# A graph layer with kernel attention: queries, keys and values taken after the first two row tiles, h kept in the place of x

## The chip, the cores and the metric

The kernel runs on one core of a Trainium2 chip. The metric is the device time of one execution in microseconds (us). Engines are named as the profile names them: PE is TensorE, DVE is VectorE, ACT is ScalarE, POOL is GpSimd, SP is SyncE, which here only issues DMAs. Each engine works through its own instructions in the order in which the program was written, and waits on semaphores.

## The reference

All of it is float32. `x` has 1250 rows (nodes) of 512 features, and there are 20000 edges, sorted by destination.

```python
h = relu(layernorm(x))                       # by row
xn = batchnorm1(h)                           # over the nodes
agg = segment_sum(xn[src], dst) / max(deg, 1)
conv = relu(agg @ W_conv + b_conv)
q, k, v = h[:256] @ Wq, h[:256] @ Wk, h[:256] @ Wv      # 8 heads of 64; only 256 positions exist
qf = exp(u(q) - diag(q) - rowmax) / 16 + 1e-6           # u = head @ proj.T, 256 features; diag = |q|^2 / 2
kf = exp(u(k) - diag(k) - max over positions and features) / 16 + 1e-6
attn = (qf @ (kf.T @ v)) / (qf @ sum(kf) + 1e-6)
h_attn = (attn @ Wo)[pos]                    # rows past 255 take row 255
out = x + batchnorm2(conv + h_attn + h)
```

Queries, keys and values need the first 256 rows of `h` alone, which are the first two tiles of 128 rows.

## The kernel before

The rows of `x` lie in ten tiles of 128 (the last has 98 rows). Loops over `i` run over these tiles, loops over `f` over four blocks of 128 features. Everything is written out by hand: the order of each engine's program is the order of its calls in the source.

**The layer norm.** DVE takes mean and variance of each tile (`ln_stats`, L832 to L837) in three groups (tiles 0 and 1; 2 to 5; 6 to 9), ACT takes the root (`ln_std_of`, L402), DVE makes scale and bias from it (`ln_scale`, L802 to L806 and L843). ACT writes h = relu(scale * x + bias) in float32 (`ln_tile`, L384) into `hring`, a ring of two tiles. From there ACT makes `h1`, the float16 of 2048 h (L389), DVE makes `h2`, the float16 rest (`split`, L848), and PE transposes the tile into a PSUM bank (`transpose_h`, L514), which ACT stores to `hT` (`store_hT`, L367). `hring` has two places, so that tile i waits until tile i-2 is split and transposed.

**Queries, keys, values.** PE multiplies columns 0 to 255 of `hT` with `wq` and `wk` (`qk`, L522, two calls each) and with `wvo` (L620). ACT stores q and k and squares them (L394, L397), from which PE takes the diagonals (`diagonal`, L550).

**The edges.** DVE counts for each window of ten destinations how many sampled edges lie below it (L821, L823, L824), PE adds this up (L506, bank "first"), DVE turns it into row numbers (L876, L879), and four indirect DMAs of POOL gather the edges (L355). DVE decodes them (L891 to L904), PE transposes the result (L570, bank "cols"; L574, bank "out"), and DVE copies that to `bcol` and `vcol` (L912, L913). Then, for each of 25 groups of windows, DVE makes two blocks of one-hot rows (`one_hots`, L870, two instructions), PE multiplies them (`count`, L537, ten matmuls) into bank 0 or 1, and ACT stores the counts (`store`, L376) to the adjacency `A16`. Aggregation is then a dense product of h1 and h2 with `A16` (`aggregate`, L611), in three chunks of 500, 500 and 250 destinations.

**The features and the attention.** PE makes u for keys (eight calls of `features` with `kT`, L629), ACT copies each (L445), DVE takes its maximum (L958), and the maxima of all keys go through PE ("kmaxT", L653; "kmax", L657). For the queries DVE takes the row maxima from the bank (`q_bias`, L992, L993), ACT takes the exponentials (L467, L468 for queries, L460 for keys), PE transposes them (`transpose_qf`, L639) into bank 7 for even heads and bank 2 for odd ones, and DVE (L1000, even) or ACT (L455, odd) stores them. A loop over pairs of heads `hp` = 0 to 3 holds this part on PE and DVE. After it PE runs `aggregate(0, FT)`, which sums the in-degrees and waits until ten groups are stored, then `aggregate(0, 0)`, then the attention (L681, L695, L709, L722) between further aggregations, and at last the convolution (L772), its batch norm and the transposes back (L787). `finish` adds x and SP writes the output.

**The first batch norm.** Its sums come from `hT` (`bn_piece`, L855, twelve instructions, and L938 to L941). Its scale and shift are made of them with a root from ACT (L437) and eight short instructions on DVE (L802 to L806, L949 to L951). `mean` (L984, L987) uses them.

**PSUM.** A list `order` gives each result its bank. `pe_open` waits until the last reader of that bank is done.

```python
            def ln_tile(i):
                if i >= 2:
                    act.wait_ge(h_split, i - 1)
                    act.wait_ge(full(("hT", i - 2)), uses[("hT", i - 2)][1])
```

## Time and profile before

| what | value |
|---|---|
| time, median of 3 runs | 210.41 us (209.47 to 214.38) |
| the profiled execution | 210.1 us |
| its span, first to last instruction | 208.3 us |
| mean granted clock of TensorE | 0.959 of full |
| PE busy | 174.3 us (84%) |
| DVE busy | 151.1 us (73%) |
| ACT busy | 73.9 us (35%) |

Busy is the time in which an engine has an instruction under way; matmuls overlap, so that a busy PE is not one at its peak. All times in the rows are counted from the span's start. 1.8 us of the profiled execution lie outside of the span.

### The profile page before, as it was taken

To read this page: it belongs to the slowest core of one execution; us is meant where nothing else is said; L and a number is where in the kernel's file an instruction comes from. 1 tells how busy PE (TensorE), PEld (TensorE's weight loads), DVE (VectorE), ACT (ScalarE), POOL (GpSimd) and SP (SyncE) were. 2 spreads that over 40 slices of the span, in tenths; PEclk is the share of its full clock that TensorE was granted. 3 is DMA by queue.
4 is the path that set the end of the run, shared out by engine and by line. 5 is a ranking of instruction groups with operands and counts; after the bars stand their busy time and mean duration, and the time that the engine had idled before them with its cause. 6 is when DMAs were issued, how large, how long until landed. Compare 5 with 4: busy or idle time off the path is not lost.

```text
span 208.3 us, 2829 instructions
## 1 busy us (share of the span) xinstructions
PE 174.3 (84%) x1072; PEld 122.8 (59%) x1072; DVE 151.1 (73%) x316; ACT 73.9 (35%) x139; POOL 6.8 (3%) x21
## 2 busy tenths in 40 slices
PE   0149989999939758999999999999986999998191
PEld 0127879756827544599956875555873444466190
DVE  5799989596989695077699989997760435265794
ACT  2074695953739893022112112111000212223560
POOL 5250000000000000000000000000000000000000
PEclk9999999999995996999999999999999999999769
DMA  5999500002300000000000000000000000000058
GB/s 187 337 322 354 192 0 3 0 0 74 148 0 0 0 5 0 0 3 0 3 0 0 0 3 0 0 3 0 0 3 5 0 0 0 3 0 0 2 203 289
DMA packets 6507, 11.13 MB, mean 53 GB/s; under 512 B 1050, under 2 KB 1376, under 8 KB 6492
## 3 DMA queue, kind: packets, MB, share of 16 engines
q1 hardware_dynamic: 6300, 10.67, 15.0%
q0 software_dynamic: 192, 0.26, 0.4%
q8 instruction: 10, 0.16, 0.4%
q14 instruction: 5, 0.04, 0.1%
HBM read 8.36 MB, written 2.56 MB: 52 GB/s over the span
## 4 chain that ended last, share of the span: by engine, by line
PE 73%; DVE 16%; ACT 6%; issue 3%; POOL 1%; DVEq 0%; ACTq 0%; POOLq 0%
PE bank L611 22%; PE bank L772 16%; PE bank L522 6%; PE bank L537 4%; PE bank L695 4%; PE bank L620 3%; PE bank L681 3%; PE bank L722 3%; DVE mxk L958 2%; PE bank L629 2%; DVE mxq L992 2%; PE bank L787 2%; DVE xs L1192 2%; PE bank L639 2%; PE bank L550 2%
## 5 line engine op out<-in xcount | busy, mean ns | idle before, releaser
L611 PE MATMUL bank<-r,h 128*128 128x500 f16 (+1 forms) x240 | 43.7, 339 | 0.0
L772 PE MATMUL bank<-r,wc 128*128 128x500 f32 (+1 forms) x96 | 33.8, 513 | 2.5 <-issue 2.5
L376 ACT ACTIVATE r<-bank 128x500 f16<-128x500 f32 x25 | 14.8, 591 | 54.1 <-PE bank L537 54.0
L611 PEld LDWEIGHTS bank<-r,h 128*128 128x128 f16 x240 | 23.0, 97 | 17.6
L772 PEld LDWEIGHTS bank<-r,wc 128*128 128x128 f32 x96 | 18.0, 189 | 18.1 <-issue 17.4
L487 ACT ACTIVATE r<-bank,vec 128x500 f32<-128x500 f32 (+1 forms) x12 | 7.3, 608 | 41.7 <-PE bank L772 41.7
L870 DVE TENSOR_TENSOR ohb<-iota,bcol 128x1280 f16<-128x1280 f16 x25 | 20.5, 819 | 2.0 <-PE bank L537 1.8
L522 PE MATMUL bank<-hT,r 128*128 128x256 f32 x64 | 16.9, 424 | 0.7 <-issue 0.7
L870 DVE TENSOR_TENSOR ohv<-iota,vcol 128x1000 f16<-128x1000 f16 x25 | 16.8, 671 | 0.0
L537 PEld LDWEIGHTS bank<-ohv,ohb 128*128 128x128 f16 x250 | 13.9, 101 | 3.6 <-issue 1.3
L537 PE MATMUL bank<-ohv,ohb 128*128 128x100 f16 x250 | 15.8, 210 | 0.0
L522 PEld LDWEIGHTS bank<-hT,r 128*128 128x128 f32 x64 | 13.5, 216 | 3.3 <-issue 1.1
L1159 DVE SCALAR_TENSOR_TENSOR r<-hT,haT,r 128x244 f32<-128x244 f32 (+2 forms) x12 | 6.7, 562 | 9.8 <-ACT r L487 9.8
L787 PE MATMUL bank<-ident,r 128*128 128x128 f32 (+1 forms) x40 | 6.9, 353 | 5.2 <-DVE r L1186 5.2
L984 DVE SCALAR_TENSOR_TENSOR r<-bank,s,r 128x500 f32<-128x500 f32 (+1 forms) x12 | 7.8, 648 | 3.9 <-PE bank L611 3.8
L514 PE MATMUL bank<-ident,hring 128*128 128x128 f32 x40 | 6.5, 307 | 4.8 <-ACT hring L384 4.8
L639 PE MATMUL bank<-ident,qe 128*128 128x128 f32 x32 | 6.2, 337 | 4.5 <-ACT r L455 4.4
L787 PEld LDWEIGHTS bank<-ident,r 128*128 128x128 f32 (+1 forms) x40 | 6.6, 188 | 5.6 <-DVE r L1186 5.6
L1158 DVE TENSOR_TENSOR r<-r,hT 128x256 f32<-128x256 f32 x4 | 1.7, 426 | 11.2 <-ACT r L487 11.2
L848 DVE SCALAR_TENSOR_TENSOR h<-hring,h 128x512 f16<-128x512 f32 x10 | 6.7, 683 | 3.2 <-ACT h L389 3.2
L384 ACT ACTIVATE hring<-xs,lnw 128x512 f32<-128x512 f32 x10 | 8.0, 803 | 2.5 <-DVE lnw L843 2.5
L1033 DVE COPY kv<-bank 128x260 f32<-128x260 f32 x4 | 1.7, 428 | 9.4 <-PE bank L681 9.4
(158 smaller groups left out, 260.6 us busy)
## 6 DMA issues: line engine op xcount, KB each, us to landing
xs<-in_x SPq DMA_DIRECT2D x9, 256.0 KB, 3.6
out<-xs SPq DMA_DIRECT2D x9, 256.0 KB
r<-in_L_gnn_Wq SPq DMA_DIRECT2D x1, 1024.0 KB, 7.0
r<-in_L_gnn_Wk SPq DMA_DIRECT2D x1, 1024.0 KB, 9.3
wvo<-in_L_gnn_Wv SPq DMA_DIRECT2D x1, 1024.0 KB, 11.5
wc<-in_L_gnn_W_conv SPq DMA_DIRECT2D x1, 1024.0 KB, 14.5
wvo<-in_L_gnn_Wo SPq DMA_DIRECT2D x1, 1024.0 KB, 5.3
xs<-in_x SPq DMA_DIRECT2D x1, 196.0 KB
```

What stands on the lines that cost most here:

```text
L376: act.activation(A16[:, :, p * GW * W:(p + 1) * GW * W].rearrange("p a (q d) -> p q a d", q=GW), bank[p % 2][:, 0:GW * NT * W].rearrange(" ...
L384: act.activation(hring[:, i % 2, :], xs[:, i, :], ACT.Relu, bias=lnw[:, 3, i:i + 1], scale=lnw[:, 2, i:i + 1]).then_inc(h_ready, 1)
L487: act.activation(yT[:, f, c0:c0 + cn], acc[:, 0:cn], ACT.Relu, bias=vec[:, 4 * V_BC + f:4 * V_BC + f + 1]).then_inc(read(("conv", c, f)), 1)
L522: last = nc.tensor.matmul(acc[:, t * NA:(t + 1) * NA], w[:, f, c:c + P], hT[:, f, 0:NA], start=(f == 0), stop=(f == FT - 1))
L537: last = nc.tensor.matmul(bank[p % 2][:, q * NT * W:(q + 1) * NT * W], ohb[:, s, :], ohv[:, s, :], start=(k == 0), stop=(k == K - 1))
L611: last = nc.tensor.matmul(acc[:, 0:cn], lhs, A16[:, s, c0:c0 + cn], start=(s == 0 and hh is not h2), stop=(s == NT - 1 and hh is not h1))
L639: last = nc.tensor.transpose(acc[:, o:o + P], qe[:, h % 4, t, m * P:(m + 1) * P], ident[:, :])
L695: last = nc.tensor.matmul(acc[:, j * (DH + 1):(j + 1) * (DH + 1)], qfT[:, m, h, t * P:(t + 1) * P], kv[:, m, h, :], start=(m == 0), stop=( ...
L772: last = nc.tensor.matmul(acc[:, 0:cn], wc[:, f, o * P:(o + 1) * P], aggT[:, f, c0:c0 + cn], start=(f == 0), stop=(f == FT - 1))
L787: last = nc.tensor.transpose(acc[0:n, f * P:(f + 1) * P], yT[:, f, i * P:i * P + n], ident[:, :])
L870: last = V.tensor_tensor(oh[:, s0:s0 + n, :].rearrange("p s (m t) -> p s m t", t=2), iota16[:, 0:size].rearrange("p (m t) -> p m t", t=2). ...
L984: V.scalar_tensor_tensor(out=aggT[:, f, c0:c0 + cn], in0=acc[:, 0:cn], scalar=s1[:, f:f + 1], in1=rdeg[:, c0:c0 + cn], op0=ALU.mult, op1=A ...
```

## The change

`hring` goes. `ln_tile` writes h over the tile of `xs` that held x. PE transposes and DVE splits from there, no tile waits for an earlier one, and the making of `h1` is a function of its own (`high_part`), called later. SP loads x once more once all tiles are transposed, halved and split, and `finish` waits for that. `asum`, which lay over `hring`, gets its own place.

On PE both calls of `qk` for the queries follow the first two transposes, then come the other tiles by pairs with one product between two pairs: the keys' two, then the first half of the values. "first" stands behind the first two transposes, "cols" and "out" behind those of tiles 6 and 7. SP loads Wq after two tiles of x and Wk after six. Of the first four calls of `count` one stays before the features of the keys, three go between them.

On DVE the layer norm of tiles 0 and 1 comes ahead of L823 and L824, all layer norms come ahead of the decoding of the edges, the splits of tiles 6 to 9 move into the loop over `hp`, the sums of the first batch norm move behind that loop, and its scale and shift stand behind the attention's last result.

The diff, without the bank list, the helpers that only change a name, and lines that repeat (the `...` lines mark what is left out):

```diff
@@ SP
+            def load_x(i):
                 n = P if i < NT - 1 else LAST
+                sp.dma_start(xs[0:n, i, :], x[i * P:i * P + n, :]).then_inc(x_in[i], 16)
+            load_x(0)
+            load_x(1)
+            sp.dma_start(wq, w_q.rearrange("(t p) n -> p t n", p=P)).then_inc(wq_in, 16)
+            for i in range(2, 6):
+                load_x(i)
+            sp.dma_start(wk, w_k.rearrange("(t p) n -> p t n", p=P)).then_inc(wk_in, 16)
...
+            landed(sp, ("hT", NT - 1))
+            sp.wait_ge(h1_ready, NT)
+            sp.wait_ge(h_split, NT)
+            for i in range(NT):
+                load_x(i)
@@ ACT
             def ln_tile(i):
-                if i >= 2:
-                    act.wait_ge(h_split, i - 1)
-                    act.wait_ge(full(("hT", i - 2)), uses[("hT", i - 2)][1])
-                act.activation(hring[:, i % 2, :], xs[:, i, :], ACT.Relu,
+                act.activation(xs[:, i, :], xs[:, i, :], ACT.Relu,
                                bias=lnw[:, 3, i:i + 1], scale=lnw[:, 2, i:i + 1]).then_inc(h_ready, 1)
-                if i not in (0, 2):
-                    store_hT(i - 1)
+            def high_part(i):
                 act.wait_ge(h_ready, i + 1)
...
             ln_tile(2)
             ln_tile(3)
-            ln_std_of(2)
             qk(0, 0)
+            qk(0, 1)
+            store_hT(2)
+            store_hT(3)
             ln_tile(4)
             ln_tile(5)
-            qk(0, 1)
+            ln_std_of(2)
...
-                if h == 2:
+                if h in (1, 3, 5):
                     store()
...
+            store()
+            act.wait_ge(bn_var, 1)
+            act.activation(bw[:, 1, :], bw[:, 0, :], ACT.Sqrt).then_inc(bn_std, 1)
             while stores[0] < NGRP:
                 store()
@@ PE
             qk("q", wq, 0)
+            qk("q", wq, 1)
             transpose_h(2)
             transpose_h(3)
-            qk("q", wq, 1)
+            pe.wait_ge(wk_in, 16)
+            qk("k", wk, 0)
+            transpose_h(4)
+            transpose_h(5)
...
+            qk("k", wk, 1)
+            transpose_h(6)
+            transpose_h(7)
...
                 last.then_inc(full(("v", t)), 1)
+                diagonal(0, t)
                 diagonal(1, t)
-                count()
+                if t == 0:
+                    transpose_h(8)
+                    transpose_h(9)
+                    count()
...
                 features("uk", kT, i)
-                if i == 1:
+                if i in (1, 3, 5):
                     count()
             features("uq", qT, 0)
             features("uq", qT, 1)
-            count()
...
-                if hp < 3:
+                count()
+                if hp == 1:
                     count()
             aggregate(0, FT)
@@ DVE, the loop over hp and behind it
-                if hp < 3:
+                one_hots()
+                if hp == 1:
                     one_hots()
+                if hp == 0:
+                    split(6)
+                    split(7)
+                if hp == 1:
+                    split(8)
+                    split(9)
+            bn1_sums()
...
                 if i % 2:
                     one_hots()
+            bn1_scale()
             in_degrees(0)
             mean(0, 0)
...
             def finish(i):
                 n = P if i < NT - 1 else LAST
                 acc = landed(dve, ("zT", i))
+                dve.wait_ge(x_in[i], 32)
```

What the lists of instructions show at three places follows. First DVE at the start, from the comparison of the sampled edges (L821 before, L840 changed) on. `r<-r` is the work on the edges, `st<-xs`, `mv<-st` and `lnw` are the layer norm. Before:

```order
L821 TENSOR_TENSOR r<-r,thr 125x1250
L823 TENSOR_REDUCE r<-r 125x125
L824 COPY r<-r 125x250
L876 TENSOR_SCALAR first<-bank 126x2
L879 TENSOR_SCALAR rows<-first,rowc 126x2
L832 BN_STATS st<-xs 128x6 x2
L835 BN_AGGR mv<-st 128x2 x2
```

Changed:

```order
L840 TENSOR_TENSOR r<-r,thr 125x1250
L849 BN_STATS st<-xs 128x6 x2
L852 BN_AGGR mv<-st 128x2 x2
...
L860 SCALAR_TENSOR_TENSOR lnw<-mv,lnw 128x2
L894 TENSOR_REDUCE r<-r 125x125
L895 COPY r<-r 125x250
L849 BN_STATS st<-xs 128x6 x4
L852 BN_AGGR mv<-st 128x2 x4
L854 TENSOR_SCALAR lnw<-mv 128x4
L898 TENSOR_SCALAR first<-bank 126x2
L901 TENSOR_SCALAR rows<-first,rowc 126x2
```

The first layer norm has moved ahead of the edges' four instructions, and the row numbers behind the second group's statistics.

Second, PE from the last product of the keys to the features of the keys (`bank<-pT,r`); `bank<-half,r` are the diagonals, `bank<-ohv,ohb` one `count`. Before:

```order
L522 MATMUL bank<-hT,r 128x256 x8
L550 MATMUL bank<-half,r 128x2 x4
L537 MATMUL bank<-ohv,ohb 128x100 x10
L514 MATMUL bank<-ident,hring 128x128 x8
L620 MATMUL bank<-wvo,hT 128x512 x4
L550 MATMUL bank<-half,r 128x2 x4
L537 MATMUL bank<-ohv,ohb 128x100 x10
L620 MATMUL bank<-wvo,hT 128x512 x4
L550 MATMUL bank<-half,r 128x2 x4
L537 MATMUL bank<-ohv,ohb 128x100 x10
L629 MATMUL bank<-pT,r 128x256 x4
```

Changed:

```order
L527 MATMUL bank<-ident,xs 128x128 x8
L605 MATMUL bank<-ident,r 128x124
...
L635 MATMUL bank<-wvo,hT 128x512 x4
L563 MATMUL bank<-half,r 128x2 x8
L527 MATMUL bank<-ident,xs 128x128 x8
L550 MATMUL bank<-ohv,ohb 128x100 x10
L635 MATMUL bank<-wvo,hT 128x512 x4
L563 MATMUL bank<-half,r 128x2 x8
L648 MATMUL bank<-pT,r 128x256 x4
L550 MATMUL bank<-ohv,ohb 128x100 x10
L648 MATMUL bank<-pT,r 128x256 x4
```

"cols" (L605) now stands directly ahead of the values, and one `count` is left ahead of the features.

Third, DVE in the loop over `hp`, from the maxima of heads 6 and 7 (`mxq<-bank`) to the store of the transposed features of head 4 (`r<-bank 128x2x256`). Before:

```order
L992 TENSOR_REDUCE mxq<-bank 128x2
L993 SCALAR_TENSOR_TENSOR qb<-mxq,diag 128x2
L870 TENSOR_TENSOR ohb<-iota,bcol 128x1280
L870 TENSOR_TENSOR ohv<-iota,vcol 128x1000
L1000 TENSOR_SCALAR r<-bank 128x2x256
```

Changed, beginning with the splits of tiles 6 and 7 (`h<-xs,h`):

```order
L865 SCALAR_TENSOR_TENSOR h<-xs,h 128x512 x2
L1013 TENSOR_SCALAR r<-bank 128x2x256
...
L1005 TENSOR_REDUCE mxq<-bank 128x2
L1006 SCALAR_TENSOR_TENSOR qb<-mxq,diag 128x2
L887 TENSOR_TENSOR ohb<-iota,bcol 128x1280
L887 TENSOR_TENSOR ohv<-iota,vcol 128x1000
L887 TENSOR_TENSOR ohb<-iota,bcol 128x1280
L887 TENSOR_TENSOR ohv<-iota,vcol 128x1000
L865 SCALAR_TENSOR_TENSOR h<-xs,h 128x512 x2
L1013 TENSOR_SCALAR r<-bank 128x2x256
```

Four splits and one more pair of one-hot rows stand ahead of the store of head 4, which frees bank 7 for the transposes of head 6.

## Rows read from the trace of the kernel before

**Rows 1.** The page, the chain that ended last: shares of the span by engine.

```profile
PE 73%; DVE 16%; ACT 6%; issue 3%; POOL 1%; DVEq 0%; ACTq 0%; POOLq 0%
```

**Rows 2.** Timeline of DVE: start, duration, line, operation; in brackets idle time and releaser.

```profile
5.17 1.46 DVE L823 TENSOR_REDUCE r<-r 125x125 f32<-125x1250 f32 x1
...
8.57 1.28 DVE L832 BATCH_NORM_STATS2 st<-xs 128x6 f32<-128x512 f32 x2
```

**Rows 3.** Timeline of ACT, tiles 0 and 1.

```profile
12.68 0.63 ACT L389 ACTIVATE h<-hring 128x512 f16<-128x512 f32 x1
13.22 0.80 ACT L384 ACTIVATE hring<-xs,lnw 128x512 f32<-128x512 f32 x1
```

**Rows 4.** Issue of Wq by SP, and its size and time to landing.

```profile
3.02 0.43 SPq L312 DMA_DIRECT2D r<-in_L_gnn_Wq  x1
...
r<-in_L_gnn_Wq SPq DMA_DIRECT2D x1, 1024.0 KB, 7.0
```

**Rows 5.** Timeline of PE, 15.9 to 60 us.

```profile
15.92 6.07 PE L522 MATMUL bank<-hT,r 128*128 128x256 f32 x16 [0.73 <-issue]
...
22.70 3.62 PE L522 MATMUL bank<-hT,r 128*128 128x256 f32 x16
...
28.56 0.21 PE L581 MATMUL bank<-ident,vrow 20*128 20x20 f32 x1 [0.62 <-DVE vcol L913]
...
45.03 0.61 PE L537 MATMUL bank<-ohv,ohb 128*128 128x100 f16 x10
45.48 3.66 PE L620 MATMUL bank<-wvo,hT 128*128 128x512 f32 x8
...
50.33 1.14 PE L629 MATMUL bank<-pT,r 64*128 64x256 f32 x8
```

**Rows 6.** Timeline of DVE, 50 to 60 us.

```profile
51.77 0.17 DVE L802 RECIPROCAL bw<-bw 128x4 f32<-128x4 f32 x1
...
53.58 1.28 DVE L958 TENSOR_REDUCE mxk<-r 128x2 f32<-128x512 f32 x2
54.78 0.82 DVE L870 TENSOR_TENSOR ohb<-iota,bcol 128x1280 f16<-128x1280 f16 x1
...
56.10 3.65 DVE L958 TENSOR_REDUCE mxk<-r 128x2 f32<-128x512 f32 x6
```

**Rows 7.** Timeline of PE, 60 to 84 us.

```profile
60.01 0.27 PE L653 MATMUL bank<-ident,mxk 128*8 128x128 f32 x1 [2.60 <-DVE mxk L962]
...
76.88 0.65 PE L639 MATMUL bank<-ident,qe 128*128 128x128 f32 x4
79.02 1.12 PE L639 MATMUL bank<-ident,qe 128*128 128x128 f32 x4 [1.49 <-ACT r L455]
79.93 3.38 PE L611 MATMUL bank<-r,c 128*128 128x500 f16 x10
```

**Rows 8.** Timeline of DVE, 70 to 90 us.

```profile
73.21 0.69 DVE L992 TENSOR_REDUCE mxq<-bank 128x2 f32<-128x512 f32 x1 [0.58 <-PE bank L629]
...
76.14 0.68 DVE L1000 TENSOR_SCALAR r<-bank 128x512 f32<-128x512 f32 x1
...
89.30 0.43 DVE L1033 COPY kv<-bank 128x260 f32<-128x260 f32 x1 [8.29 <-PE bank L681]
```

**Rows 9.** The instructions on `hT`: ns min/median/max, first and last start, forms.

```profile
L855 DVE BATCH_NORM_STATS2 st<-hT x12: 375/675/686, 33.5 to 44.6; 128x6 f32<-128x512 f32 x8, 128x6 f32<-128x226 f32 x4
```

**Rows 10.** Timeline of DVE and of PE, 113 to 120 us.

```profile
113.99 1.28 DVE L1051 COPY qe<-bank 128x512 f32<-128x512 f32 x2
...
115.53 3.69 PE L722 MATMUL bank<-qe,wvo 128*128 128x256 f32 x16
```

**Rows 11.** Windows: length, busy of PE, PEld, DVE, ACT, POOL; PEclk, DMA share, GB/s.

```profile
60.00:65.00 5.00, 4.29 (x17) 2.85 (x18) 4.18 (x13) 4.16 (x9) 0.00 (x0) 0.67 0.00 0
...
75.00:80.00 5.00, 2.74 (x23) 2.29 (x24) 5.00 (x8) 4.45 (x11) 0.00 (x0) 0.88 0.02 5
```

**Rows 12.** Timeline of DVE, the first of the edges' decoding (20.6 us).

```profile
20.62 0.29 DVE L891 TENSOR_SCALAR r<-r 126x256 int32<-126x256 int32 x1
```

160 lines of the change are left out of this document (72 added, 88 removed), and 3 rows, old and new, of the table order.

## The prediction

> **What bounds the kernel now.** I read the chain that ended last first: 73% of it is PE, 16% DVE, 6% ACT [rows 1]. So a step counts if it moves PE's instructions, and I then followed PE's timeline and looked at every wait in it. It has three parts. Up to 15.9 us PE is starved: the first product of the queries starts at 15.92 [rows 5]. The reader is to see what lies ahead of it: DVE works on the sampled edges from 5.17 and comes to the layer norm's statistics only at 8.57 [rows 2]. From 15.9 to 50.3 us PE is nearly never idle. From there to the in-degrees' sum (the first `aggregate`) at 79.93 it waits for DVE and ACT, for 2.60 us ahead of the keys' maximum at 60.01 and for 1.49 ahead of 79.02 [rows 7]. Then it is full to the last `mean`, with DVE close behind it. The change works on the first two parts and pays for that in the third and behind it.
>
> **The change part by part.** All times are of the profiled execution, 210.1 us, of which 208.3 are span. It lies 0.3 under the median of the runs, 210.41, and the last step adds that.
>
> *The start.* The statistics of tiles 0 and 1 start where L823 does, at 5.17 instead of 8.57: 3.4 earlier, if x is there. I take it that it is, as DVE went through these two without idling. On ACT the first `h1` (0.63, at 12.68) stood between the two relus; its successor starts 0.54 behind it [rows 3], and the second relu now comes that much sooner. The first product starts at 15.92 - 3.4 - 0.5 = 12.0. Wq was issued at 3.02 and took 7.0 to land [rows 4], which is 10.0; it is now issued two transfers sooner, so that it doesn't bind. Gain **3.9**; least 1.9 (Wq as late as 14.0), most 4.0.
>
> *From the first product to the keys' features* there are 50.33 - 15.92 = 34.4 us [rows 5]. Three of four `count` leave it; one advances PE by 45.48 - 45.03 = 0.45, together 1.35. They aren't saved but moved to where PE waits anyway. The wait of 0.62 ahead of the vectors' transpose at 28.56, for DVE's `vcol`, has no successor there, since "cols" comes later now. The first product is slow: 6.07 against 3.62 for the same 16 matmuls at 22.70 [rows 5], and the next one too if the clock stays low for as long. I leave that cost of 2.45 as it is. So 34.4 - 1.35 - 0.6 = 32.4, and the features start at 44.4, **5.9** earlier than before. By bounds this part gives 0 (new waits as long as what goes) to 4.4 (the slow start gone as well). The Trainium skill, "TensorE: Matmul & The Clock Gate", section "Part 1: The HAM clock gate", says that PE begins throttled and that activity releases it; by this rule too the low stretch starts with PE's work and goes along with it, the sum staying as it is, while thin PE work later would lower the clock again, which is the third rival below.
>
> A new tie stands here. ACT takes the root of the third group only behind both stores of the queries, `store_hT` 2 and 3 and two relus; DVE waits for it in `ln_scale`, and the edges' decoding, "cols" and `vcol` are queued behind this wait. I put it at 0 and price it under the fourth rival.
>
> *The features of the keys.* DVE goes over eight heads with one pair of one-hot rows from 53.58 on, up to 56.10 + 3.65 = 59.75, and the keys' maximum follows on PE at 60.01 [rows 6, 7]. Now three pairs stand there, each 56.10 - 54.78 = 1.32. But DVE no longer comes late from the batch norm: it may start once the first key is copied, 1.2 after the features start (two features 1.14 [rows 5], half of that, and a copy of about the 0.6 of DVE's instructions on this size), at 45.6. 45.6 + 6.2 + 2.6 + 0.2 = 54.6 against 60.0. Of the 5.9 this leaves 5.4; **cost 0.5**.
>
> *The loop over `hp`.* Until here PE has won 5.4. The stretch from 60.01 to 79.93 is a ring of ACT, PE and DVE. DVE gets four splits and two pairs of one-hot rows more. Two splits are about 1.2: the nearest row is two DVE instructions over 128x512 that take 1.28 and overlap the next by a little [rows 2]. In the first pass they stand ahead of the maxima of head 6, where DVE idled 0.58 ahead of 73.21 [rows 8]; so DVE comes 0.6 late. In the second pass a pair (1.32) and two splits (1.2) stand ahead of the store of head 4, which was at 76.14 and took 0.68 [rows 8]: it ends at 76.82 + 0.6 + 2.5 = 79.9. This frees bank 7 for the transposes of head 6, which ran at 76.88 and now at 80.0, those of head 7 right behind them (before at 79.02 [rows 7]), until 80.9. Then, and this is new, PE has a `count` (0.45) and ACT its `store` (0.6) ahead of the in-degrees' sum, which needs ten groups: 82.1 against 79.93. **Cost 2.2**. Lower bound 1.05, the last two alone; upper 1.05 and all that DVE gets, 2.6 + 2.4, so 6.1. I take 2.2 because each wait in it is that of a named bank.
>
> *The first batch norm.* Its twelve instructions on `hT` are at most 12 x 0.675 = 8.1 [rows 9] and overlap to some 7.0 with what follows. Before, DVE idled 8.29 ahead of 89.30 [rows 8]. In the loop it gets 5.0 more work, of which 0.6 filled a wait; PE itself is 2.2 late; so 2.2 of that idle time go, 6.1 are left for 7.0, and the first `kv` copy comes 0.9 late. Only L695, four products later, needs that copy, and DVE is faster than PE there. Cost nothing, 1.0 if this cover fails. ACT waits for these sums with its stores behind it; by the same count it has over 2 us. Its scale and shift took from 51.77 to 53.58 less a copy, 1.6 [rows 6], and now stand ahead of the in-degrees on DVE, which has no idle time there: the copies of `attnT` end at 113.99 + 1.28 = 115.27 and PE takes them at 115.53 [rows 10]. Cover 0.3, **cost 1.3**; bounds 0 and 1.6.
>
> *The rest.* x again is ten transfers after the last split (about 75 us); the share of the DMA engines is 0.00 to 0.02 there [rows 11], and it is needed past 198 us. The extra root on ACT falls where ACT idles. Both nothing; were x late, SP's outputs would be late with it.
>
> **Sum:** -3.9 - 2.0 + 0.5 + 2.2 + 1.3 = -1.9. 210.1 - 1.9 = 208.2, and with the 0.3 to the median **208.5 us**.
>
> **The rivals.**
> 1. *The forecast*, 208.5, own range 206.3 to 210.8.
> 2. *The loop hides what it gets.* For: PE is busy 2.74 of 5 us there at 75 to 80 [rows 11], and the ring has waits in it that the splits could fill; if ACT and not DVE sets its pace, 1.05 is left of 2.2, and the batch norm's 1.3 is absorbed in the many one-hot rows made ahead. Against: DVE is busy 5.00 of 5.00 in that window. 210.4 - 5.4 + 1.05 = 206.1, and 204.5 where the clock's fall at the loop's end is spared as well (below, 1.2, and a little).
> 3. *TensorE's clock falls for longer*, the slower side. In the window 60 to 65 the granted clock was 0.67, behind the idle 2.60 us, and 0.88 at 75 to 80 behind thin work; the sum that followed took 3.38 for ten matmuls [rows 7, 11], whose later ones come at 0.21 each, so 1.2 lost. The loop is now 2.2 longer with about the same PE work in it, and it ends in aggregates, where PE is the bound. If half the clock (1.2 instead of 2.4 GHz) covers 7 us of those, 3.5 is lost, of which 0.5 was so before: 208.5 + 3.0 = 211.5. [...] Against: the stretch before had the same shape.
> 4. *The tie of "cols".* First product 12.0 + 6.07, the second 3.6, two stores with squares, two `store_hT`, two relus and the root, some 3.8, put the root at 25.4; scale 1.2, decoding 3.8, two splits and the vectors' copy 1.4: 31.8. PE comes to "cols" at about the same time. Before, DVE began the decoding at 20.62 [rows 12]; the gather is now started 5 us later, behind other loads, so it may be there at 25.7 and is needed at 26.6. Each microsecond later goes straight to PE; at 3 us 211.5.
> 5. *The start doesn't come forward*, because x or Wq lands late: 2 us less, 210.5.
>
> **How the numbers follow.** Chances: 0.50 the forecast, 0.25 the second, 0.13 the third, 0.07 the fourth, 0.05 the fifth. The range leaves out the upper bound of the loop with the low clock together (over 213) and the second rival with every cover (under 204.2): 204.2 to 212.8. Two per cent is 4.2 us, about what a measurement of this kernel tells from no change; its own runs are 209.5 to 214.4. Under 206.2 lie the second rival for the most part and a tail of the first: 0.26. Above 214.6 only the third with the loop's upper bound: 0.06. The rest, 0.68, is no change.
>
> **What the changed profile would show.** The first product of the queries near 12.0 and the keys' features near 44.4. The keys' maximum on PE near 54.6. The in-degrees' sum near 76.7, 22 us behind it instead of 19.9, with PE waiting for DVE's store of head 4 ahead of the transposes of head 6. L722 some 2.0 us earlier than 115.53, with a wait of about a microsecond ahead of it. No wait ahead of the `finish` instructions. The prediction is wrong if "cols" has a wait of over 1 us, if the loop takes under 21 or over 24 us, or if the granted clock is low in the aggregates for more than one slice of the page.

## The result and the profile after

The changed kernel took 214.98 us (median of 4 runs, 213.58 to 215.53) beside 209.94 for the kernel before (4 runs, 209.41 to 214.38): ratio 1.0238, 95% interval 1.0165 to 1.0312: slower, though the interval leaves open whether by more than 2%. The forecast was 208.5, its range ended at 212.8. The kernel was run again later on another chip: 214.24 (6 runs, 213.46 to 216.06) beside 210.79, ratio 1.0153, 1.0100 to 1.0207. The profiled execution of the first set took 215.37 with a span of 213.5. Executions of one kernel lie some 2 to 7 us apart here; the ratios leave out those far above the fastest of their kernel, the medians below do not, and the traces of four experiments (counts twice, one-hot rows early, scale early, edges first) are of such executions.

The start of the same piece of work on PE, in us from the span's start, is the account that matters. "Again" is the second trace of the changed kernel; the last three columns are experiments that follow.

| starts on PE | before | changed | again | splits early | four moves | moves, counts |
|---|---|---|---|---|---|---|
| first product of the queries | 15.92 | 12.03 | 12.03 | 12.33 | 12.20 | 12.23 |
| features of the keys | 50.33 | 45.40 | 44.77 | 44.34 | 45.43 | 44.51 |
| the keys' maximum | 60.01 | 57.70 | 57.08 | 56.09 | 55.41 | 54.49 |
| in-degrees' sum | 79.93 | 80.25 | 81.69 | 78.64 | 76.47 | 77.20 |
| first product of keys and values | 87.36 | 89.53 | 89.64 | 84.98 | 84.20 | 83.54 |
| product with Wo | 115.53 | 119.28 | 119.39 | 114.74 | 112.36 | 111.71 |
| convolution | 157.86 | 161.63 | 162.09 | 157.03 | 154.09 | 151.42 |
| transposes of the output | 196.90 | 202.20 | 202.81 | 196.06 | 193.12 | 190.38 |
| end of the span | 208.3 | 213.5 | 214.2 | 207.5 | 204.7 | 201.7 |

So the changed kernel is 4.9 us ahead at the keys' features, 2.3 ahead at their maximum, 0.3 behind at the in-degrees' sum and 5.2 behind at the end. The page of the changed kernel has, in the granted clock of 40 slices and in the chain that ended last:

```profile
PEclk9999999998899795999999999999996999999979
...
PE 65%; DVE 24%; ACT 5%; issue 4%; POOL 1%; DVEq 0%; ACTq 0%; POOLq 0%
```

VectorE's share of the chain rose from 16% [rows 1] to 24%: it was on the path for 33 us and is now for 51. The clock is lowest in the 16th slice (80.1 to 85.4 us) and in the 31st (160.1 to 165.5). The PE timeline shows the places; these answer to [rows 5, 7, 10]:

```profile
12.03 10.08 PE L535 MATMUL bank<-hT,r 128*128 128x256 f32 x32
...
32.80 0.63 PE L605 MATMUL bank<-ident,r 124*128 124x124 f32 x4 [0.62 <-DVE vec L929]
...
45.40 1.14 PE L648 MATMUL bank<-pT,r 64*128 64x256 f32 x8
...
49.97 0.62 PE L550 MATMUL bank<-ohv,ohb 128*128 128x100 f16 x10 [1.81 <-DVE ohv L887]
...
57.70 0.27 PE L671 MATMUL bank<-ident,mxk 128*8 128x128 f32 x1 [1.18 <-DVE mxk L957]
...
68.83 0.83 PE L658 MATMUL bank<-ident,qe 128*128 128x128 f32 x4 [2.76 <-ACT r L472]
...
77.90 1.09 PE L658 MATMUL bank<-ident,qe 128*128 128x128 f32 x8 [2.18 <-DVE r L1013]
...
80.25 4.35 PE L626 MATMUL bank<-r,c 128*128 128x500 f16 x10 [0.81 <-ACT r L383]
84.39 5.30 PE L626 MATMUL bank<-r,h 128*128 128x500 f16 x20
89.53 1.90 PE L700 MATMUL bank<-v,r 128*128 128x65 f32 x16
...
117.89 0.62 PE L550 MATMUL bank<-ohv,ohb 128*128 128x100 f16 x10 [0.52 <-DVE ohv L887]
119.28 3.69 PE L741 MATMUL bank<-qe,wvo 128*128 128x256 f32 x16 [0.77 <-DVE qe L1073]
```

The start is as forecast. Behind the start of the keys' features PE no longer waits once for VectorE, as before, but three times: twice for one-hot rows of a `count` that stands between two features (1.81 and 0.81), then for the maximum (1.18). The two aggregates at 80.25 take 9.28 us to the next product; in [rows 7] the first of them took 3.38 where it now takes 4.35. The chain of waits says who set the pace ahead of the maximum (start, us, what; 46 to 56 us):

```profile
46.62 0.60 ACT r L462
...
47.32 1.28 DVE mxk L953 x2
48.60 0.73 DVE ohb L887
49.33 0.59 DVE ohv L887
49.92 1.19 DVE mxk L953 x2
51.11 0.73 DVE ohb L887
51.84 0.60 DVE ohv L887
...
52.48 1.01 PE bank L550 x10
53.50 2.02 PE bank L648 x7
...
55.54 0.61 ACT r L462
...
56.17 1.29 DVE mxk L953 x2
```

VectorE does, up to 52.44. Then PE does: it waited for the one-hot rows, its clock has fallen (0.71 of full in the window 50 to 55 us), and the last features of the keys take 2.02 instead of 1.14. VectorE's own timeline shows what it did ahead of all this; compare [rows 6, 8]:

```profile
45.50 0.19 DVE L949 COPY diag<-bank 128x32 f32<-128x32 f32 x1 [7.14 <-PE bank L563]
47.32 1.28 DVE L953 TENSOR_REDUCE mxk<-r 128x2 f32<-128x512 f32 x2 [1.62 <-ACT r L462]
...
56.17 1.28 DVE L953 TENSOR_REDUCE mxk<-r 128x2 f32<-128x512 f32 x2 [1.23 <-ACT r L462]
...
83.27 6.01 DVE L872 BATCH_NORM_STATS2 st<-hT 128x6 f32<-128x512 f32 x12
...
91.46 0.43 DVE L1054 COPY kv<-bank 128x260 f32<-128x260 f32 x1 [1.21 <-PE bank L700]
```

It stood still for 8.8 us just where it ran out of work, because splits and batch norm had been moved behind the maxima. That is the reading I missed: work was taken out of a place where VectorE then idles, and put where everything waits for VectorE. Last, the windows of the changed kernel (columns as in [rows 11]), of the two aggregates and of the convolution's first 8 us:

```profile
80.25:89.53 9.28, 9.28 (x31) 3.77 (x32) 9.24 (x19) 1.24 (x1) 0.00 (x0) 0.68 0.68 221
161.63:169.63 8.00, 8.00 (x16) 3.65 (x17) 1.49 (x3) 0.68 (x1) 0.00 (x0) 0.81 0.01 2
```

The same stretches before had a clock of 0.85 and 1.00 and took 7.43 us and 19 matmuls in 8 us.

### The profile page after: what moved, and what is told of

The parts are those of the page before. It is cut to its first block, busy times and chain, and to the rows that moved or that the text cites. A ratio compares the mean times of both kernels' runs of the same rounds, so it can differ in the third digit from the quotient of the medians.

```text
span 213.5 us, 2843 instructions
## 1 busy us (share of the span) xinstructions
PE 176.7 (83%) x1072; PEld 122.6 (57%) x1072; DVE 151.3 (71%) x316; ACT 74.2 (35%) x139; POOL 7.2 (3%) x21
## 4 chain that ended last, share of the span: by engine, by line
PE 65%; DVE 24%; ACT 5%; issue 4%; POOL 1%; DVEq 0%; ACTq 0%; POOLq 0%
PE bank L626 18%; PE bank L791 17%; PE bank L535 5%; PE bank L714 3%; PE bank L741 3%; PE bank L700 3%; PE bank L635 3%; PE bank L648 3%; PE bank L550 3%; DVE ohb L887 3%; DVE ohv L887 2%; DVE mxq L1005 2%; DVE mxk L953 2%; PE bank L806 2%; PE bank L563 2%
## 5 line engine op out<-in xcount | busy, mean ns | idle before, releaser
L626 PE MATMUL bank<-r,h 128*128 128x500 f16 (+1 forms) x240 | 44.6, 343 | 0.0
L791 PE MATMUL bank<-r,wc 128*128 128x500 f32 (+1 forms) x96 | 35.4, 530 | 2.5 <-issue 2.5
L791 PEld LDWEIGHTS bank<-r,wc 128*128 128x128 f32 x96 | 18.7, 196 | 19.0 <-issue 18.4
L527 PE MATMUL bank<-ident,xs 128*128 128x128 f32 x40 | 6.1, 304 | 9.4 <-ACT xs L388 9.4
L527 PEld LDWEIGHTS bank<-ident,xs 128*128 128x128 f32 x40 | 5.3, 159 | 9.6 <-issue 9.3
L658 PE MATMUL bank<-ident,qe 128*128 128x128 f32 x32 | 4.9, 288 | 7.1 <-ACT r L472 3.8
L806 PE MATMUL bank<-ident,r 128*128 128x128 f32 (+1 forms) x40 | 6.3, 334 | 5.2 <-DVE r L1208 5.2
L806 PEld LDWEIGHTS bank<-ident,r 128*128 128x128 f32 (+1 forms) x40 | 6.0, 176 | 5.6 <-DVE r L1208 5.6
L992 DVE RECIPROCAL r<-r 128x500 f32<-128x500 f32 (+1 forms) x3 | 8.2, 2746 | 0.0
L1000 DVE SCALAR_TENSOR_TENSOR r<-has_in,t,r 128x500 f32<-128x500 f32 (+1 forms) x12 | 7.8, 653 | 0.4
```

The lines of the kernel that those rows point to most:

```text
L527: last = nc.tensor.transpose(acc[:, f * P:(f + 1) * P], xs[:, i, f * P:(f + 1) * P], ident[:, :])
L626: last = nc.tensor.matmul(acc[:, 0:cn], lhs, A16[:, s, c0:c0 + cn], start=(s == 0 and hh is not h2), stop=(s == NT - 1 and hh is not h1))
L791: last = nc.tensor.matmul(acc[:, 0:cn], wc[:, f, o * P:(o + 1) * P], aggT[:, f, c0:c0 + cn], start=(f == 0), stop=(f == FT - 1))
L806: last = nc.tensor.transpose(acc[0:n, f * P:(f + 1) * P], yT[:, f, i * P:i * P + n], ident[:, :])
L992: link(V.reciprocal(rdeg[:, c0:c0 + cn], rdeg[:, c0:c0 + cn]))
L1000: V.scalar_tensor_tensor(out=aggT[:, f, c0:c0 + cn], in0=has_in[:, 0:cn], scalar=t1[:, f:f + 1], in1=aggT[:, f, c0:c0 + cn], op0=ALU.mult, ...
```

## The experiments

Two theories. **V**: VectorE's new order costs the time. **C**: TensorE's low clock does, which falls on stretches that are PE's alone. A third, D, is that the second load of x collides with something.

**Splits early.** The changed kernel, with one part undone: the splits of tiles 6 to 9 leave the loop for VectorE's idle time.

```diff
+            for i in range(6, NT):
+                split(i)
             acc = landed(dve, "diag")
...
-                if hp == 0:
-                    split(6)
-                    split(7)
-                if hp == 1:
-                    split(8)
-                    split(9)
```

> The changed kernel with the splits of tiles 6 to 9 moved on VectorE from the loop over hp to the place ahead of the diagonals' copy, where VectorE idled 7.14 us. Theory V (the loss is VectorE's order: it idles 8.8 us ahead of the keys' maxima and is then the bound up to the in-degrees' sum): the splits stood ahead of the maxima of head 6 (1.2 us, of which VectorE's wait of 1.62 behind them hides a part) and ahead of the store of head 4 (1.2 us in the open), so the in-degrees' sum comes 1.5 to 2.4 us sooner and the whole is 1.5 to 2.5 us shorter than the changed kernel. Theory C (the loss is TensorE's low clock: 3.4 us stretches at 52, 69, 79 to 86 and 161 us): under 0.7 us, unless the low stretches move, and a change of several us only together with theirs.

210.66 us (4 runs, two at 209 and two at 212 to 213) beside 210.63 for before: 4.3 less than the changed kernel, where V had said 1.5 to 2.5 and C under 0.7, or several us together with the low stretches. Its VectorE and PE:

```profile
40.40 1.29 DVE L865 SCALAR_TENSOR_TENSOR h<-xs,h 128x512 f16<-128x512 f32 x2 [1.90 <-ACT h L393]
44.45 0.19 DVE L951 COPY diag<-bank 128x32 f32<-128x32 f32 x1 [2.75 <-PE bank L563]
46.26 1.28 DVE L955 TENSOR_REDUCE mxk<-r 128x2 f32<-128x512 f32 x2 [1.62 <-ACT r L462]
```

```profile
78.64 2.28 PE L626 MATMUL bank<-r,c 128*128 128x500 f16 x10 [0.81 <-ACT r L383]
80.76 4.38 PE L626 MATMUL bank<-r,h 128*128 128x500 f16 x20
84.98 1.90 PE L700 MATMUL bank<-v,r 128*128 128x65 f32 x16
```

The splits cost nothing at their new place, and the keys' maximum comes 1.6 sooner, of which 1.1 are there at the features already. But the loop without them takes 22.55 us up to the in-degrees' sum, to the hundredth what it took with them, at a granted clock of 0.77 where the changed kernel had 0.91. The window of the changed kernel:

```profile
57.70:80.25 22.55, 13.91 (x120) 10.31 (x120) 20.12 (x41) 19.10 (x44) 0.00 (x0) 0.91 0.09 24
```

What this trace wins behind the maximum are the aggregates, 6.34 us at the full clock for 9.28 and 7.95 in the changed kernel's two traces, and the convolution, 1.5. These 4.5 us are C's condition: a change of several us together with the low stretches. So the time fits neither theory by itself, and this run doesn't show what the splits cost in the loop.

**Counts twice.** The changed kernel with the counts of groups 1 to 9 run twice, which leaves the result as it is and adds 0.45 us of PE work each.

```diff
-                for q in range(GW):
+                for again in range(2 if 1 <= p <= 9 else 1):
+                  for q in range(GW):
                     for k in range(K):
```

> The changed kernel with the ten matmuls of each count run twice for the groups 1 to 9, the second time over the first, so that TensorE has 9 x 0.45 = 4.0 us more work in the stretch from the keys' features to the in-degrees' sum, where it waits for 11 us. Theory V: the work lies partly in waits, partly ahead of stores that the ring needs; the whole is 0.5 to 2.5 us longer than the changed kernel. Theory C: the granted clock no longer falls between 52 and 86 us, which gives back 1.3 us in the features and 1.9 us in the first aggregates and more in the loop: 1 to 3 us shorter than the changed kernel in spite of the added work.

212.47 (10 runs, 210.34 to 213.81), ratio to before 1.0060, 1.0007 to 1.0114: 2.5 and 1.8 below the changed kernel's two medians, with 4 us more PE work in it. That is C's number and against V, though the interval of this ratio meets that of the second set at its edge (1.0100 to 1.0114). The windows from the features to the maximum, of the loop and of the aggregates:

```profile
44.93:56.36 11.43, 8.48 (x101) 6.54 (x101) 9.32 (x17) 6.00 (x11) 0.00 (x0) 1.00 0.26 97
...
56.36:80.48 24.12, 17.73 (x179) 14.25 (x180) 20.54 (x41) 19.21 (x44) 0.00 (x0) 0.86 0.09 29
80.48:86.82 6.34, 6.34 (x30) 3.02 (x31) 6.34 (x11) 1.25 (x1) 0.00 (x0) 1.00 0.86 297
```

From the features to the maximum it is 11.43 us at the full clock, where the changed kernel's two traces have 12.30 at 0.86 and 12.31 at 0.75. The loop got longer by 1.6 (24.12 for 22.55) and the aggregates shorter by 2.9, at the full clock. C has a real part in it. But C had also said that the clock no longer falls between 52 and 86 us, and it did: it was 0.53 from 60 to 65, and 0.79 in the convolution's first 8 us. Nor do the aggregates of one trace prove much, since the splits early had the full clock there without more PE work. Of the eleven traces with single counts two have it, and all three with doubled ones. The DMA engines were busy here for 0.86 of the aggregates' window (0.68 of the longer one in the changed kernel), so the reload of x beside the aggregates doesn't slow them; that speaks against D.

**No reload.** The changed kernel without the second load of x. Its last addition takes h in the place of x, so the output is another one.

```diff
-            landed(sp, ("hT", NT - 1))
-            sp.wait_ge(h1_ready, NT)
-            sp.wait_ge(h_split, NT)
-            for i in range(NT):
-                load_x(i)
...
-                dve.wait_ge(x_in[i], 32)
```

> The changed kernel without the second load of x: the output adds h in the place of x, so this part is left out. Theory D (ten transfers at 77 to 86 us collide with the loop's end and the first aggregates): the stretch from the loop to the first product with kf gets 1 to 2 us shorter. Theories V and C: nothing, within 0.5 us.

213.59 (4 runs, 212.16 to 214.39), ratio to before 1.0118, 1.0002 to 1.0234. That is 0.7 to 1.4 below the changed kernel and within the spread of both. In its trace the aggregates took 6.85 us, 1.1 to 2.4 less than in the changed kernel, which is what D had said; but they ran at a clock of 0.92 for 0.68 and 0.79, and the counts twice had 6.34 with the reload beside them, so that the clock is enough to explain it. Transposes of the output to the end take 11.4 us with the reload and without. D is worth 1.4 us at most by the medians, and that isn't resolved.

**Start only.** The kernel before with the start of the changed one: the layer norm of tiles 0 and 1 ahead of the edges' sum on VectorE, "first" behind two transposes on PE, Wq after two tiles.

```diff
+            ln_stats(0)
+            ln_scale(0)
             link(V.tensor_reduce(nbelow[:, :], below[:, :, :], AX_X, ALU.add))
...
             transpose_h(0)
             transpose_h(1)
+            pe.wait_ge(nb_ready, 1)
+            acc = pe_open(pe, "first")
```

> The kernel before with the start of the change alone: the layer norm of tiles 0 and 1 ahead of the edges' reduction, the product for the first rows behind the first two transposes, Wq loaded after two tiles of x. The first product of the queries starts at 12.4 to 13.0 instead of 15.92 us. Theory S (a gain at the start reaches the end as long as what follows keeps its order): 2.5 to 3.5 us shorter than the kernel before. Rival (TensorE isn't the bound between 15.9 and 50 us, since ScalarE, VectorE and the hring ring follow their own clock, or the edges' gather now comes too late): under 1 us shorter, with new waits for the ring or the edges on TensorE before 30 us.

215.85 (4 runs, 214.53 to 216.64), ratio 1.0227, 1.0109 to 1.0344: slower by as much as the whole change, which neither theory had. The first product starts at 12.48, 3.4 sooner, and the keys' features at 53.96, 3.6 later. PE and VectorE in between:

```profile
12.48 5.72 PE L515 MATMUL bank<-hT,r 128*128 128x256 f32 x16
...
27.38 1.10 PE L570 MATMUL bank<-ident,r 124*128 124x124 f32 x4 [2.88 <-DVE r L903]
```

```profile
23.49 0.29 DVE L890 TENSOR_SCALAR r<-r 126x256 int32<-126x256 int32 x1 [1.78 <-DMA r<-in_dst,rows]
```

The gather of the edges is started 4.2 us later and lands at 23.5, where before VectorE took its result at 20.62 without a wait [rows 12]. In PE's old order the edges' transposes stand in the middle of the start, and everything behind them waits. The clock was low there too (0.68 from 25 to 30 us and 0.63 from 30 to 35), and the next run is to part the two.

**Edges first.** The same with the edges' sum and "first" left ahead.

```diff
             link(V.tensor_reduce(nbelow[:, :], below[:, :, :], AX_X, ALU.add))
             V.tensor_copy(nbelow4[:, :, :], ...).then_inc(nb_ready, 1)
+            ln_stats(0)
+            ln_scale(0)
             dve.wait_ge(full("first"), uses["first"][1])
```

> The kernel before with only the start changed, as in the run that took 215.9 us, but the sampled edges' chain left ahead: VectorE sums the comparison before the first layer norm, and TensorE's first two matmuls stay in front of the transposes. The rows of the gather are then ready at about 10.7 (8.4 in before, 12.6 in that run). If that run lost by the late gather, the decoding starts at 21.4 here (20.6 before, 23.5 there), the first product at 14.4 (15.9 before), and the time is 210 to 212. The rival: what it lost is the earlier and thinner start of TensorE itself (its clock was low from 26.8 to 33.7 there, in the middle of the products); then 213.5 or more here as well.

212.81 (12 runs, 210.01 to 214.22), ratio 1.0023, 0.9977 to 1.0069: the late gather's number by the ratio (some 211), between the two by the median. First product 14.30, decoding 21.50, as expected, but the features of the keys come at 53.33, only 0.6 sooner than with the start only. PE:

```profile
25.39 0.65 PE L570 MATMUL bank<-ident,r 124*128 124x124 f32 x4 [1.56 <-DVE r L903]
...
28.94 0.26 PE L581 MATMUL bank<-ident,vrow 20*128 20x20 f32 x1 [1.44 <-DVE vcol L912]
...
29.61 6.00 PE L522 MATMUL bank<-hT,r 128*128 128x256 f32 x16
```

The account to the features is -1.6 from the start, +2.4 from waits (3.0 for 0.62 before) and +2.4 from one product at the low clock (6.00 for 3.62). So in the trace both answers hold: PE that starts sooner arrives sooner at the edges and waits there, and behind the waits its clock is low (0.56 in the window 30 to 35 us; 1.00 before). The Trainium skill, page "TensorE: Matmul & The Clock Gate", section "HAM oscillation — how this bites in real kernels", describes this: a PE that waits for its data goes back to the low clock and begins the next block slowly. The trace agrees, with 6.00 us for 3.62, though its waits, 1.56 and 1.44 us, are shorter than those that the page shows (some 3 to 5).

**One-hot rows early.** Splits early, and one pair of one-hot rows more moved ahead of the diagonal's copy.

```diff
             for i in range(6, NT):
                 split(i)
+            one_hots()
             acc = landed(dve, "diag")
...
-                if h in (1, 3, 5):
+                if h in (3, 5):
                     one_hots()
```

> This is the run with the four splits ahead of the diagonal's copy (210.7 us; in it the keys' maximum is transposed at 56.09) with one thing more: the third pair of one-hot rows, which now stands between VectorE's maxima over the keys, is made ahead of the diagonal's copy too. Theory V (VectorE's order): VectorE idles from 41.7 to 44.5 and from 44.6 to 46.3 there, so 1.4 of one-hot rows cost nothing at that place and leave the stretch in which TensorE waits for the maxima: the transpose comes 1.3 us earlier, at about 54.8, TensorE's wait of 1.81 for one-hot rows at 48.92 goes, and 0.8 to 1.3 of it reaches the end: 209.4 to 209.9. Theory C (the low clock of TensorE decides): the maximum comes earlier as well, but the loop behind it is paced by low stretches (59.9 to 63.3, 66.7 to 73.6 in that run) which the edit doesn't take away: 210.3 to 211, with as many low us as before.

211.90 (8 runs, 208.33 to 215.01), ratio 0.9986, 0.9914 to 1.0057. The maximum comes 10.0 us behind the features instead of 11.8, which is 1.8 where V had said 1.3. The clock has a part in that: it was 1.00 in this stretch for 0.85 with the splits early. PE:

```profile
54.15 0.27 PE L671 MATMUL bank<-ident,mxk 128*8 128x128 f32 x1 [1.25 <-DVE mxk L960]
```

PE's wait for the maximum is as long as before (1.25 for 1.29), and one of the two waits for one-hot rows is gone. The same stretch takes 9.98 us at the full clock in both later runs that hold this edit, so it is no matter of one execution. The end doesn't show it: in this trace the loop behind it took 23.6 for 22.6 and the aggregates 9.3 for 6.3. As a time of its own this run is inconclusive.

**Scale early.** Splits early, and the batch norm's scale ahead of the attention blocks.

```diff
+            bn1_scale()
             for i in range(4):
                 t, half = divmod(i, 2)
                 acc = landed(dve, ("attn", i))
...
-            bn1_scale()
             in_degrees(0)
```

> The run with the four splits early (210.7 us) with the first batch norm's scale and shift (eight small VectorE instructions, 1.75 us) moved from behind the four attention blocks to ahead of them. The prediction priced their place in the changed kernel at 1.3 us. If that is right, TensorE's waits of 0.52 (for one-hot rows at 113.34) and 0.77 (for the copy of attnT at 114.74) go and the product with Wo starts 1.3 earlier, at 113.4, for 209.4. The rival: VectorE is late at the attention blocks instead (its idle times there are 0.82 and 0.95, against 1.75 put in), TensorE waits as long a little earlier, and the time stays at 210.4 to 210.7.

210.72 (10 runs, 209.01 to 214.07), ratio 1.0006, 0.9970 to 1.0042. PE at the place:

```profile
116.36 0.61 PE L550 MATMUL bank<-ohv,ohb 128*128 128x100 f16 x10
116.85 3.48 PE L741 MATMUL bank<-qe,wvo 128*128 128x256 f32 x15
```

Both waits, 0.52 and 0.77, are gone, and from the first product of keys and values to that with Wo it is 28.17 us, to the hundredth what it was before; it was 29.75. So the term of 1.3 was right. The median alone would not have shown it.

**Flag early.** Splits early, and PE reads the flag of coverage ahead of the last five aggregates.

```diff
+            pe.wait_ge(flag_ready, 1)
+            covered = pe.value_load(flag[0:1, 0:1], min_val=0, max_val=1)
             for f in DEG_FIRST:
                 aggregate(2, f)
-            pe.wait_ge(flag_ready, 1)
-            covered = pe.value_load(flag[0:1, 0:1], min_val=0, max_val=1)
```

> The run with the four splits early (210.7 us) with TensorE's reading of the flag of coverage moved ahead of the last five aggregates, so that only the branch stands in the gap of 2.42 us ahead of the convolution (157.03). Theory C: that gap is what lets the clock fall in the convolution of the changed kernel (low from 161.3 to 164.8, right behind a gap of 2.47 us; transposes back 40.6 us after the convolution's start instead of 39.0). If the reading makes up the gap, it shrinks to about 1 and no run of this kernel falls low there; 1 to 1.5 us faster, 209.2 to 209.7. The rival: the gap is the branch and the loading of the code behind it, it stays at 2.4, and the time stays at 210.7; then the gap can't be what the edit moves, and the fall of the clock at the convolution stays a matter of each run.

210.38 (10 runs, 208.23 to 213.61), ratio 0.9974, 0.9922 to 1.0027. The gap went from 2.42 to 1.78, and another releaser is named:

```profile
156.28 1.92 PE L791 MATMUL bank<-r,wc 128*128 128x500 f32 x4 [1.78 <-DVE r L1002]
```

0.6 won; most of the gap isn't the reading.

**Counts twice in the kernel before.** The same doubled counts, there.

> The kernel before, with the counts of groups 1 to 9 run twice (same result, 0.45 us more TensorE work each at full clock, 4 us in all). In the changed kernel the same edit took 2.5 us off. Theory C (thin work of TensorE lets its clock fall, and the changed kernel is thinner than the one before in the loop over the heads): before has three low stretches behind its start, 61.7 to 68.5, 78.8 to 82.2 and 194.8 to 201.6; the counts near the first two fill TensorE, and the time is between 208.5 and 210.5, not slower. Theory V (order of VectorE alone): TensorE waits for VectorE only ahead of the keys' maximum and in the loop, three to four of the nine counts lie in waits and the other five cost 0.45 each: 212 to 213.

212.45 (4 runs, 212.01 to 213.91), ratio 1.0133, 1.0081 to 1.0185: V's number, but not V's way. The three doubled counts in front of the features cost 1.3 us. The loop and the aggregates behind it gave back 1.7 (19.36 for 19.92 and 6.32 for 7.43), so that the product with Wo starts at 115.15, 0.4 sooner than before, with the added work done. What is lost in this trace lies behind that: 1.4 in the convolution, at 0.82 in its first 8 us, and 0.9 in the last stretch, from 198.16 on. That a convolution so far behind is slow because of the doubled counts isn't shown. So denser PE work doesn't pay here as a whole, and where PE waits it does.

**Again.** The changed kernel itself.

> The changed kernel itself once more, beside the other three on one chip, because single executions of one kernel lie up to 6 us apart here and its variants' low stretches fall at other places each time. Theory V (order): all its executions are late, since the keys' maximum and the batch norm's scale are late in each: median 213.5 to 215.5, the fastest over 212. Theory C (the low clock falling on the aggregates and on the convolution in the profiled execution by chance): a spread as wide as that of the run with the splits early (208.9 to 212.9) and a fastest one below 211.5.

214.24, the fastest 213.46. No execution came near the 208.9 of the run with the splits early. The loss is steady, as V said. But the low clock is as steady: the mean granted clock was 0.920 to 0.926 in these six executions, 0.942 to 0.959 in those of the kernel before beside them. So this run speaks against a low clock that falls by chance, not against one that the new order brings.

**Four moves.** The three single moves and the splits together.

> The changed kernel with the four moves of the single runs together: splits of tiles 6 to 9 and one pair of one-hot rows ahead of the diagonal's copy, the batch norm's scale ahead of the attention blocks, the flag read ahead of the last aggregates. By theory V the parts add, as milestones on TensorE showed them one at a time: 1.8 from the features to the keys' maximum for the one-hot rows, of which the loop lets about 1 through, 1.6 from the first product of keys and values to the product with Wo, 0.6 ahead of the convolution, all against the run with the splits early (fastest 208.85, median 210.66): fastest near 206, median 207.5 to 208.5, faster than both kernels. Theory C: the low stretches inside the loop and at the aggregates take up what is gained (thinner work of TensorE beside a faster VectorE): median 209.5 to 211, with a low stretch on the aggregates in the profile.

207.50 (6 runs, 206.21 to 209.73), ratio to before 0.9827, 0.9771 to 0.9884; V's number. It beats both kernels, and is 6.7 us below the changed kernel on the same chip. The loop and the aggregates:

```profile
55.41:76.47 21.06, 14.02 (x119) 10.58 (x119) 18.21 (x37) 19.10 (x44) 0.00 (x0) 0.91 0.02 6
76.47:84.20 7.73, 7.73 (x30) 3.37 (x31) 7.73 (x14) 1.25 (x1) 0.00 (x0) 0.82 0.00 0
```

Here the loop can be compared with the changed kernel's, since the clock is the same (0.91): 21.06 for 22.55. How much hangs on that clock is seen in the run with the one-hot rows early, whose program is the same up to here: 23.59 at 0.77. The aggregates ran at a low clock for part of the time all the same.

**Four moves and counts.** That, with the counts of the five groups in the loop run twice.

> The four moves, and the counts of the five groups in the loop over the heads run twice (same result; 0.45 us more of TensorE each at full clock, where TensorE waits for VectorE and ScalarE anyway). Theory C: denser work there spares the low stretch that falls on the loop's second half or on the aggregates (worth 1.7 to 3.4 us where it falls on them): median 1 to 2 us below that of the four moves alone. Theory V: the loop is set by VectorE and ScalarE, the extra counts are hidden or cost up to 1 us: the same median or up to 1 us more.

205.01 (6 runs, 203.49 to 206.47), ratio 0.9734, 0.9682 to 0.9786, the fastest of all. C asked for a median 1 to 2 us lower and it is 2.5 lower, and V had said the same or up to 1 us more; but the trace gives the clock little of it. The window of the aggregates and the start of the convolution:

```profile
77.20:83.54 6.34, 6.34 (x31) 3.02 (x32) 6.34 (x11) 1.25 (x1) 0.00 (x0) 1.00 0.01 3
```

```profile
142.88 8.70 PE L627 MATMUL bank<-r,h 128*128 128x250 f16 x80
151.42 1.84 PE L792 MATMUL bank<-r,wc 128*128 128x500 f32 x4
```

The aggregates won 1.4, the loop lost 1.65 (22.71 for 21.06), and the gap ahead of the convolution, 1.86 in the four moves, is not there at all, which is worth 2.0. The rest is the start, 0.9. What removed the gap wasn't tried. It wasn't VectorE's last `mean`, which the profile names as releaser in the four moves: here the convolution starts at 151.42, ahead of that instruction (152.13). The traces point at the fetching of instructions (last section).

## Why the prediction was wrong

It forecast 208.5 and measured 214.98; the account is that of the profiled executions, +5.2 on PE's path where -1.9 was forecast.

*The start*, -3.9: measured -3.89. Right, with its reason. But "start only" shows that this gain is worth nothing by itself. I take it that it survives to the keys' features because the change also moves "cols" behind the tiles; no run moved "cols" alone.

*From the first product to the keys' features*, -2.0: measured -1.0, and -1.7 in the second trace. The tie of "cols", put at 0, cost 0.62, and the slow start, left as it was, took 0.4 more (10.08 for 32 matmuls, where 6.07 and 3.62 stand in [rows 5]). The prediction took that slowness for the clock's. The profile doesn't show it: the granted clock reads 1.00 from 12 to 22 us, and from 15.9 to 22 in the kernel before, while the DMA engines are busy throughout (shares of 1.0 and more). What slows these products stays open.

*The features of the keys*, +0.5: measured +2.6 in both traces. This is the step that failed first. The prediction had "45.6 + 6.2 + 2.6 + 0.2 = 54.6". VectorE began at 47.32, not at 45.6. The features were 1.0 later than forecast, and ScalarE's first copy starts 1.2 behind them (46.62), not 0.6; VectorE waits for it, and the diagonal's copy is done before. And from there to the maximum it wasn't 8.8 but 10.2: VectorE's own work was as forecast, 8.9, and 1.2 is its wait at 56.17 for ScalarE, behind features that PE did slowly after two waits for one-hot rows. The sum counted VectorE's work and left out that it, PE and ScalarE now take turns. At the full clock (counts twice) the stretch takes 11.4 where 10.2 was forecast and 12.3 measured, so that at least 0.9 of the 2.1 is the clock and the rest the hand-overs.

*The loop over hp*, +2.2: measured +2.6 to the in-degrees' sum, and PE waits 2.18 ahead of the transposes at 77.90 for VectorE's store, where it was forecast to. The four moves split the term: without splits in it the loop took 21.06, 1.5 under the changed kernel at the same clock. That is 1.1 over before, near the lower bound of 1.05 for the last count and store, though before ran at a clock of 0.80. In the second trace the whole was 4.7, at a clock of 0.71.

*The aggregates behind the loop*, 0: measured +1.85 and +0.5. This is the third rival's mechanism, at the place it named, held at 3.0 and a chance of 0.13. The doubled counts bear it out: in all three traces with them the aggregates have the full clock and take 6.3 us, and in two of the eleven others. It had been 7.43 before, so that the change brought 0.5 to 1.9 and the rest was there already.

*The first batch norm*: sums 0, right (VectorE still waited 1.21 for PE at 91.46); scale +1.3, measured 1.58, of which the move of the scale gave back 1.59.

*The reload of x*, 0: 0.7 to 1.4 by the medians, within the spread and so not resolved; no `finish` waited for it.

*The convolution*, not in the sum: +1.5 and +1.7. Its first 8 us ran at 0.81 of the full clock, or 0.79 in the second trace. Of the other eleven experiments six were late there in the same way and five were not. It goes with the gap of PE ahead of it: the five traces with the shortest ones (0 to 2.45) have the clock full, eight of the nine with 2.47 to 2.96 have it low. The border between 2.45 and 2.47 is too fine to be a cause, no run set that gap alone, and the cause stays open.

So the error of 7.1 us in the traces has two halves. The steps on which VectorE's order acts were 3.8 too cheap (1.0 + 2.1 + 0.4 + 0.3, of which 0.4 is the slow start and 0.9 the clock in the features), and the clock in the aggregates and in the convolution, taken as 0, was 3.4. They aren't independent: order alone (four moves) took off 6.7 us in the median, more than the 3.5 to 5.0 that the change had cost, and denser PE work alone took off 1.8 to 2.5. The fourth rival was true and small: VectorE stood for 6.59 us until the root came at 25.91. The second, a loop that hides its work, was false: VectorE was busy for 18.15 of the 20.00 us ahead of the in-degrees' sum.

None of the three signs of being wrong came up in the first trace: "cols" waited 0.62, the loop took 22.55, and one slice of the page was low in the aggregates. They watched the rivals' places, and none watched the stretch between the features and the maximum, where the sum failed first. In the second trace the loop's 24.61 was one.

## What to carry to other kernels

When work is moved off a busy engine's early program, look up how long that engine will idle where the work stood; if it then idles, as here for 8.8 us, the move has bought nothing and is paid for at the place where it lands. Add up a stretch in which three engines take turns from its hand-overs, not from the work of one. And read a change of two per cent from the start times of the same instructions in two traces, since a term of 1.3 us stands there to a few hundredths when the median of ten runs can't tell it from nothing. That holds for stretches with the same granted clock: the same loop took 21.06 and 23.59 us at 0.91 and 0.77.

## What the runs showed of the hardware

The low clock doesn't stand at the same place in two executions of one program: the two aggregates took 9.28 and 7.95 us in two traces of the changed kernel, with a granted clock of 0.68 and 0.79 of full (between the levels of 2.4 and 1.2 GHz), and 6.34 where it was 1.00. The Trainium skill, page "TensorE: Matmul & The Clock Gate", section "Part 1: The HAM clock gate", says of a kernel's start that the count of slow matmuls differs from run to run; here it is so in the middle of the kernel too. The time of an execution goes with its mean clock: of 17 executions of the kernel before on one chip, the 13 up to 211.7 us have 0.958 or 0.959, and three of the four over 212 have 0.942. The four of the changed kernel in the first set are the exception (215.37 at 0.950, 213.58 at 0.926).

Useless PE work made a kernel faster: nine counts done twice took 1.8 to 2.5 us off the changed kernel (ratio to before 1.0060, for 1.0238 and 1.0153). It went with the full clock where PE had waited between the features (1.00 for 0.86 and 0.75).

The gap of 2.4 to 3.0 us at the branch ahead of the convolution, in which the profile names no wait, was 1.8 with the flag read earlier, and 0 with the flag read earlier and five counts doubled, far ahead, in the loop; with nine counts doubled and the flag read late it was 2.5. The traces list the fetches of instructions as DMAs of their own, and these go with the gap. In all thirteen traces that have it one fetch (queue q8) starts 2.5 to 3.0 us ahead of the convolution, however long the gap, and the next within 1.3 us behind its start. In the one trace without the gap no fetch stands at that place; there is one 0.8 to 1.0 us ahead. So the likely reading is that PE waits for the code behind the branch, and that reading the flag earlier starts this fetch earlier; the doubled counts, which make the program longer, may have moved that code. No run tests this.
